# Output projection summed in DRAM by accumulating transfers, four sums of a tile moved to VectorE where a set begins, and halves made earlier

## The reference

```python
def _L0_xattn_ref(hidden_states, cross_attention_states, ...):   # 32 heads, 8 kv heads, head_dim 128
    q = (hidden_states @ q_proj_w.T) ...; k = (cross_attention_states @ k_proj_w.T) ...; v = (... @ v_proj_w.T) ...
    q = rmsnorm(q, q_norm_w); k = rmsnorm(k, k_norm_w)            # k, v repeated for 4 query heads each
    attn = softmax(q k^T * scale + mask); out = attn v
    return out @ o_proj_w.T                                       # 4096 -> 1024
def _L0_ffn_ref(x, A, B, Wr):
    scores = x @ Wr.T; top 16 of 64, softmax -> gates G
    h = einsum('nd,krd->nkr', x, A); out = einsum('nkr,kdr->nd', h * G[:, :, None], B) * 2
x = x + tanh(g_xattn[0]) * _L0_xattn_ref(_layernorm(x), ctx, ...)
x = x + tanh(g_ffn[0]) * _L0_ffn_ref(_layernorm(x), A, B, Wr)
```

## Time and profile before

| what | value |
|---|---|
| median of 3 runs | 2366.77 us |
| the profiled execution, whole | 2371.98 us |
| its span in the profile | 2370.2 us |
| TensorE busy | 2282.6 us, 96% |
| VectorE busy | 1623.7 us, 69% |
| ScalarE busy | 1173.3 us, 50% |
| POOL busy | 1326.6 us, 56% |
| chain that ended last | TensorE 84%, VectorE 5%, POOL 4%, issue 4%, DMA 2% |
| mean granted TensorE clock | 0.987 |

### The profile page before, as it was taken

One profiled execution on the slowest core, in us unless ns is written; L12 is line 12 of the kernel. 1 busy time (PEld: TensorE's weight loads), 2 busy tenths in 40 slices (PEclk: granted clock), 3 DMA queues, 4 the chain that ended last, 5 costly groups with the idle time before them and its releaser, 6 DMA issues.

```text
span 2370.2 us, 35675 instructions
## 1 busy us (share of the span) xinstructions
PE 2282.6 (96%) x11600; PEld 1918.3 (81%) x11600; DVE 1623.7 (69%) x2649; ACT 1173.3 (50%) x3751; POOL 1326.6 (56%) x1823
## 2 busy tenths in 40 slices
PE   5998998999999989999999899999999999999899
PEld 4886887888888878888888788788787887888687
DVE  6557557777777787777777855856757878553755
ACT  4546455666666676666666722423324334333421
POOL 5566658656565556565555645655645765434321
PEclk8999999999999999999999999999999999999999
DMA  4687547657657367652222647556355467324543
GB/s 171 218 226 271 185 149 243 211 168 196 196 160 196 119 211 187 193 137 93 92 92 82 209 138 238 163 189 219 129 209 195 152 213 265 109 71 162 218 163 133
DMA packets 180231, 412.98 MB, mean 174 GB/s; under 512 B 12176, under 2 KB 77968, under 8 KB 164624
## 3 DMA queue, kind: packets, MB, share of 16 engines
q1 hardware_dynamic: 175440, 379.24, 46.9%
q0 software_dynamic: 4608, 31.46, 7.5%
HBM read 293.21 MB, written 178.26 MB: 199 GB/s over the span
## 4 chain that ended last, share of the span: by engine, by line
PE 84%; DVE 5%; POOL 4%; issue 4%; DMA 2%; ACT 1%; SPq 0%; POOLq 0%; ACTq 0%; DVEq 0%
PE bank L750 23%; PE bank L752 23%; PE bank L751 23%; PE bank L808 4%; PE bank L816 2%; DVE t_lo L1281 2%; PE bank L796 2%; PE bank L833 1%; PE bank L832 1%; PE bank L831 1%; DVE s_lo L1281 1%; DMA staged<-in_w_q 1%; POOL staged L1737 1%; ACT t_hi L991 1%; POOL s_hi L1747 1%
## 5 line engine op out<-in xcount | busy, mean ns | idle before, releaser
L750 PE MATMUL bank<-t_hi,s_hi 128*128 128x512 f32 x2688 | 1093.9, 407 | 68.0 <-DVE t_lo L1281 22.7
L752 PE MATMUL bank<-t_hi,s_lo 128*128 128x512 f32 x2688 | 1061.9, 395 | 0.0
L751 PE MATMUL bank<-t_lo,s_hi 128*128 128x512 f32 x2688 | 1059.6, 394 | 0.0
L750 PEld LDWEIGHTS bank<-t_hi,s_hi 128*128 128x128 f32 x2688 | 512.7, 191 | 173.0 <-issue 60.2
L1281 DVE TENSOR_TENSOR s_lo<-staged,s_hi 128x512 fp32r<-128x512 f32 x672 | 544.2, 855 | 99.7 <-ACT s_hi L1002 90.2
L752 PEld LDWEIGHTS bank<-t_hi,s_lo 128*128 128x128 f32 x2688 | 510.9, 190 | 112.5
L751 PEld LDWEIGHTS bank<-t_lo,s_hi 128*128 128x128 f32 x2688 | 512.9, 191 | 91.7
L1002 ACT CAST s_hi<-staged 128x512 fp32r<-128x512 f32 x434 | 250.3, 623 | 333.2 <-DMA staged<-heads 157.9
L1720 POOL TENSOR_SCALAR small<-small 128x4 f32<-128x4 f32 (+1 forms) x192 | 70.7, 368 | 411.7 <-ACT small L1091 332.6
L1735 POOL TENSOR_TENSOR staged<-staged 128x512 f32<-128x512 f32 x96 | 142.7, 1486 | 258.6 <-DMA staged<-gated 89.7
L1407 DVE SCALAR_TENSOR_TENSOR probs<-bank,small,mask 128x128 f32<-128x128 f32 x512 | 144.1, 343 | 89.9 <-POOL small L1727 43.8
(11 more groups left out here) (133 smaller groups left out, 2988.4 us busy)
## 6 DMA issues: line engine op xcount, KB each, us to landing
heads<-heads SPq DMA_DIRECT2D x128, 256.0 KB, 3.7
staged<-in_w_q SPq DMA_DIRECT2D x32, 768.0 KB, 5.6
staged<-heads SPq DMA_DIRECT2D x32, 768.0 KB, 5.8
t_raw<-in_sets SPq DMA_DIRECT2D x22, 1024.0 KB, 8.7
t_raw<-combos SPq DMA_DIRECT2D x19, 1024.0 KB, 9.7
sums<-sums SPq DMA_DIRECT2D x18, 1024.0 KB, 7.9
sums<-sums SPq DMA_DIRECT2D x36, 512.0 KB, 4.8
xt<-x_columns SPq DMA_DIRECT2D x8, 1792.0 KB, 7.0
```

Of the source, the lines that this page charges most:

```text
L750: nc.tensor.matmul(out, s_hi[w][:, cols], high, start=start, stop=False, skip_group_check=True)
L751: nc.tensor.matmul(out, s_hi[w][:, cols], low, start=False, stop=False, skip_group_check=True)
L752: done = nc.tensor.matmul(out, s_lo[w][:, cols], high, start=False, stop=at == 3, skip_group_check=True)
```

## The change

Five edits. (1) In the O phase, entries 48 to 71 no longer load and add: their results are written plainly to `sums` (three tiles by VectorE, the one of beat 4 by ScalarE), and POOL issues one accumulating 1 MB transfer from SBUF to DRAM per entry, in beat 1 of the next entry; x is put there beforehand by 16 transfers DRAM to DRAM of 512 KB in the query phase. The last eight entries add in SBUF as before, with one load of 1 MB each. (2) For the first entries of six sets (8, 56, 64, 72, 80, 88) the four sums of the streamed tile go from POOL to VectorE, in beat 4 of the entry before. (3) At turns the halves of the next entry's first four streamed tiles are made in beats 4 and 5 instead of 5 and 6, and the resident halves of the sets of entries 8, 16, 80 and 88 from beat 2. (4) The load of `staged` stands ahead of the refills of resident tiles in SP's queue. (5) In the beginning VectorE makes `t_raw1` and `t_raw6`, too, and no longer waits for POOL.

In the diff, `turn_sums` and the code with `sums_tile` are VectorE's, `stage` before `refill` is SP's (shown for the KV phase, alike in the others), and `sums_out` and the last piece are POOL's.

```diff
-FILL_POSITIONS = (4, 5, 6, 7, 9, 10, 11)
+FILL_POSITIONS = (2, 4, 5, 6, 7, 8, 9)
 FILL_POSITIONS_AHEAD = (1, 2, 3, 4, 7, 8, 9)
...
     def before_next(e, j):
         order, count = plan.a_order(plan.next(e)) if plan.next(e) else (), len(entries[e].ks)
-        return {count - 2: order[:2], count - 1: order[2:4]}.get(j, ())
+        first = count - 3 if plan.last_of_set[entries[e].tau] == e else count - 2
+        return {first: order[:2], first + 1: order[2:4]}.get(j, ())
...
+    def summed_at_turn(e):
+        return plan.first_of_set[entries[e].tau] == e and entries[e].tau in (1, 5, 6, 7, 8, 9)
...
+        def turn_sums(e, j):
+            if e + 1 == ENTRIES or j != 4 or not summed_at_turn(e + 1):
+                return
+            at = plan.sums[e + 1] - 4
+            dve.wait_ge(st_in, 16 * (plan.order[e + 1] + 1))
+            nc.vector.tensor_tensor(staged[:, 2, :], staged[:, 3, :], staged[:, 6, :], ALU.subtract).then_inc(s_sum, 1)
...
+            nc.vector.tensor_tensor(staged[:, 5, :], staged[:, 4, :], staged[:, 1, :], ALU.add).then_inc(s_sum, 1)
...
         for e in range(KV0, QA0):
             for j in SEVEN:
-                refill(e, entries[e].ks[j])
                 if j == 1:
                     stage(e + 1, e)
+                refill(e, entries[e].ks[j])
...
+    def in_dram(q):
+        return q < 24
+    def added_before(q):
+        return min(q, 24 + q % 2) // 2
...
-                if j in (3, 4, 5):
+                if j in (3, 5) and in_dram(q):
+                    sums_tile(q, j)
+                if j in (3, 4, 5) and not in_dram(q):
                     add_sums(q, j)
...
+        def sums_out(q):
+            b, e = q % 2, O0 + q
+            for c, k in ((0, 4), (2, 5), (3, 6)):
+                pool.wait_ge(taken[c], plan.after[e, k])
+            if q == 0:
+                pool.wait_ge(sums_set, 256)
+            if q >= 2:
+                pool.wait_ge(acc_out[b], 16 * added_before(q))
+            nc.gpsimd.dma_start(d.sums[pair_of(q)], acc[b][:, :, :], accum_op=ALU.add, max_dma_last_dim=8192).then_inc(acc_out[b], 16)
...
         for e in range(O0 + 2, A0):
             for j in SEVEN:
                 finish(plan.beat0[e] + j)
-                if j == 1:
+                if j == 1 and in_dram(e - O0 - 1):
+                    sums_out(e - O0 - 1)
+                if j == 1 and not in_dram(e - O0):
                     add_sums(e - O0, j)
```

179 lines of the change are left out of this document (77 added, 102 removed).

## The result

The changed kernel takes 2332.24 us (median of 4 runs, 2331.68 to 2334.57), the kernel before 2367.03 us in the same comparison (2365.5 to 2369.6): ratio 0.9854, 95% interval 0.9837 to 0.9871, so 34.8 us less. The profiled executions differ by 40.1 us (spans 2370.2 and 2330.1), since that of before lay 5.2 us above its median. Forecast were 2325 us, and a range of 2307 to 2347.

A forecast was written before the change was run, and what follows sets the result against it. Only what makes TensorE wait or slows its clock counts, with VectorE bounding every turn. Terms -6 -6 -2 -8 -15 -10 = -47, 5 us kept back: 2366.8 - 42 = 2325 us, range 2307 to 2347.

The forecast's parts named there:

- Start, -6: Entry 0: VectorE's new order without waiting for POOL starts product 1 at 36 instead of 39; -6 us, bounds -3 and -8.
- Turn 7 to 8, -6: Entries 7 to 8: own sums and earlier halves bring entry 8's products 1, 4 and 6 sooner; -6 us, bounds -2 and -9.
- rival (a): At the turns transfers become the new bound, so gains shrink to -24 us, total 2343; chance 0.15.
- 15 to 16, -2 (a third of the neighbour): Entries 15 to 16: POOL keeps its sums, `staged` comes one transfer earlier; -2 us, bounds +1 and -4.
- 31 to 32 and 47 to 48, -4 each: Query turns: `staged` loaded earlier lets POOL begin its sums five us sooner; -4 us each, bounds -1 and -6.
- with the clock behind it: Query turns: the 2.68 us wait goes and the slow clock after it too, making -4 of each 9.7 us excess.
- O turns, -15: Turns 55, 63, 71: less contention and earlier halves on VectorE's list; -4, -6, -5 of 17.4 us, bounds -6 and -17.
- 79 and 87, -5 each: Turns 79 and 87: halves made earlier, VectorE with more other work; -5 us each, bounds -2 and -8 each.
- O phase outside turns, 0: Steady O entries: TensorE busy 38.08 of 38.08 us, so fewer POOL sums and the accumulating transfers change nothing; cost 0.
- Rival (b): O entries: accumulating transfers delay every streamed tile, 3 us in each of 22 entries, total 2391; chance 0.09.
- The 5 us kept back: Whole sum: -47 cut to -42 for small POOL operations meeting `t_lo` and waits nobody is late for yet.

The follow-up runs named there:

- best2: Changed kernel with two key-tile moves on TensorE, streamed halves later at turn 8, and entry 7's streamed load behind product 1's refill: 2328.84 us, ratio 0.9842.

## Why the prediction was right, and where its sizes were off

The bound was named rightly for the start and the O turns, VectorE's list; at the query turns it was the order of SyncE's queue, which the prediction named, too. Outside turns and start nothing was gained or lost (-0.2), and the windows moved, most of them to where it put them.

- **The waits.** The prediction took the row `t_lo`, 22.7 us in 4 waits, for the turns; all four stand in the start. What the turns lost to `t_lo` stood under `issue`, 22.5 us, which it passed over. Its conclusion, that VectorE's halves are late, is right all the same, for a row that it had not read.

- **Start, -6.** The lists gave product 1's start at 36 and, at the low clock, its end near 41; the trace has 36.42 and, at the full clock, 39.4. Product 5 follows at 41.1 (forecast 42.3), and entry 0 ended at 46.93, in one other trace of this start at 46.9, and in ten, where the lower clock does fall on product 1, at 48.3 to 49.4, where 49 was forecast. The sum was right; the -8.1 of the profiled pair, just outside its bound of -8, hold 1.5 to 2.5 us of luck. In the timed runs the start is worth some 7.
- **Turn 7 to 8, -6.** Measured -4.0 (7 and 8: -6.0, 9: +2.1). The steps inside the two entries held: entry 8 starts 23.8 us behind entry 7 (23.5 before), its product 1 begins 3.1 us in instead of 6.5 and product 6 23.4 instead of 29.0; these are 3.4 and 5.6 us, forecast 3.5 and 5 to 7. Only product 4 gained 2.9 instead of 4. What the sum lacked is entry 9: its product 2 takes 5.5 us instead of 3.5, with a wait of 1.73 for GpSimd's `k_normed`, which no term had. Transfers are late at this turn, at DMA share 0.81, as rival (a) has it, but not at its price: `t_raw0` was issued at 175.1 and landed at 186.6, so the half that was to be made in beat 2 came with beat 5, and still 6.0 us were gained, not 2.
- **15 to 16, -2 (a third of the neighbour).** Measured -0.2. Entry 15 and 17 gave 2.6, entry 16 lost 2.4 to the 5.63 us wait for `k_normed`, 2.97 before. Earlier subtractions on VectorE fell on GpSimd's small operations. The term was a share of a neighbour with no list of its own, and it shows.
- **31 to 32 and 47 to 48, -4 each.** Measured -2.8 each, and by the run with edit 4 undone all of it from this edit. The steps hold: `staged` was to be issued 5.6 us into entry 31 and summed 18.0 us in; the trace has 815.68 and 827.80, so 5.8 and 18.0. DMA queue and GpSimd of entry 31, then TensorE in 32:

```profile
815.68 1.01 SPq L493 DMA_DIRECT2D staged<-in_w_q  x1
...
827.80 1.29 POOL L1741 TENSOR_TENSOR staged<-staged 128x512 f32<-128x512 f32 x1
...
843.06 1.13 PE L791 MATMUL bank<-keys,queries 128*128 128x128 f32 x8 [1.47 <-DVE probs L1410]
845.21 0.63 PE L799 MATMUL bank<-ident,probs 128*128 128x128 f32 x4 [1.02 <-DVE probs_t_lo L1269]
```

  The size failed at "with the clock behind it": the wait of 2.65 us at the start of entry 32 went and the clock is 1.00 instead of 0.98, but 2.8 us in all were gained; next in line are the attention's own waits (1.47 us for `probs`, 1.02 for its low half), and 6.9 us of excess remain. `t_lo`, which I named as next, is not it.
- **O turns, -15.** Measured -15.9, and the list for 63 to 64 held: four sums 1637.40 to 1640.0 are 14.8 to 17.4 us into the entry (forecast 15.1 to 17.8 by 1660.5 and 1663.2), `staged` landed 7 us after issue (forecast 7.7). But the shares were wrong, and the total owes that to luck. I gave the larger part to the order of the halves with VectorE's own sums; the runs give 7.0 to edit 1, whose additions I had counted as 0.68 us and "1 to 4 us in all" of contention, 5.4 to the halves, 1.0 to VectorE's sums (8.2 for the last two together).
- **79 and 87, -5 each.** Measured -3.2 and -3.3. At 79 the two beats moved were to give up to 5.4; the resident places alone are 2.5. Entry 87 became 1.2 longer and 88 and 89 shorter by 4.5; with the scatter there no more can be said. Each is within its bounds and two thirds of its term, which was a choice between bounds and not a list.
- **O phase outside turns, 0.** Right: 38.08, and 0 to plain transfers.
- **Rival (b)** did not come true, and its mechanism is shown: at 12.5 and 17.3 us of landing an entry takes 4.6 and 9.7 us more.
- **The 5 us kept back.** The terms add to -47, the profiled difference is -40.1 and that of the medians -34.8. The reserve was right for the traces; the other five are the profiled execution of before, which lay that far above its median. A forecast made against one execution should allow for such places: the start alone differs by 2.6 us between traces of one code.

What stays open: 1.4 us of the turn 7 to 8; which part of edit 1 gives its 7.0 us, GpSimd's additions, VectorE's or the loads; and why GpSimd's `ranks` and the clock differ in entries 87 to 90 between kernels with the same code there.

## What to carry over

When two engines are late together at a turn, work out separately what each piece of work costs the *other* engine: here additions of 128x512 that nobody waited for, three an entry on GpSimd and one on VectorE, were worth 7.0 us together with their loads, and moving the four sums that stood in the chain 1.0. A tile loaded earlier gives nothing while its consumer's place in an in-order list stands behind something else (best2), and what a place moved earlier wins can be lost an entry later on another engine (resident halves at 7 to 8: 2.4 us won, 1.75 lost in entry 9): list both for every moved step. Where the waits view says "issue", look in the timeline for what ended just before; here it was the second largest loss. And before more traffic is put on a shared queue, find the landing time at which the stream starts to wait, by doubling the traffic once.

## What the runs showed of the hardware

- An operation of GpSimd on 128x4 takes 0.20 us alone and took 2.11 and 2.12 when it started within 0.3 us behind the start of a VectorE subtraction of 128x2048 that takes 2.3: it ended with it. In entry 16 two of a chain of five such operations did, 3.8 us, and TensorE stood 5.63 us for what follows the chain.
- Accumulating into DRAM from SBUF: 1 MB lands in 7.8 us in the median, a plain store in 4.2. A load of 768 KB issued 1.8 to 5.0 us behind the first of one, two or three accumulating transfers lands after 6.7, 12.5 and 17.3 us, 4.8 to 5.8 more for each further one. Behind a plain one, 5.1 us behind in most entries and so when that had landed, it takes 4.6. In entry 58 with two of them, 191 of the 544 packets of the streamed tile's loads had run when the last accumulating one was done (1594.05); the rest followed in 2 us.
- Issued from GpSimd, these transfers were held up by no subtraction of VectorE: in entry 63, where VectorE makes its `t_lo`, one landed after 7.82 us, in the steady entries 65 and 66 after 8.03 and 8.55. The Trainium skill (SBUF — State Buffer, "Who interferes with whom") has such a transfer stalled by VectorE's two-port operations and not by tensor_tensor; VectorE runs tensor_tensor there, and the 7.82 us agree.
